# Redistributing a weight-quantization side stream over the four attention tiles of a two-layer transformer kernel

## What is computed

```python
xn = layernorm(x)
# layer 0: causal-weighted linear attention plus an int4-quantized linear layer with LoRA
scores    = (xn Wq^T)(xn Wk^T)^T * scale * exp(log_decay * dist) * causal
x = x + (scores @ (xn Wv^T)) Wo^T * out_scale + xn @ int4(kernel) + bias + (xn a) b
xn = layernorm(x)
# layer 1: decayed linear attention plus a feed-forward layer with ternary weights
Wq1, Wq2 = clip(round(W / (mean|W| + eps)), -1, 1)      for W1 (4096x1024), W2 (1024x4096)
x = x + attention(xn) + relu(xn Wq1^T + b1) Wq2^T + b2
```

## Time and profile before

| | us |
|---|---|
| two timed runs | 1556.30, 1684.81 (median 1620.56) |
| profiled execution, its time | 1558.54 |
| its span, slowest core (core 3) | 1557.0 |
| spans of the other seven cores | 1527.7 to 1549.3 |
| layer-0 attention, tile 0 to the start of layer 1 | 375.3 to 780.5 |
| PE busy | 1241.0 (80%) |
| ACT busy | 474.3 (30%) |
| DVE busy | 417.9 (27%) |

### The profile page before, as it was taken

How to read it: one execution, slowest core, us unless ns; L and a number is a source line. 1 busy time by engine, 2 the same in 40 slices (tenths; PEclk the granted TensorE clock), 3 DMA queues, 4 the chain that set the end, 5 groups by cost and what they waited for, 6 DMA issues and landing times. The chain is left out here.

```text
span 1557.0 us, 15405 instructions; the slowest of 8 cores (1527.7 to 1557.0 us)
## 1 busy us (share of the span) xinstructions
PE 1241.0 (80%) x5440; PEld 534.8 (34%) x5440; DVE 417.9 (27%) x704; ACT 474.3 (30%) x550; POOL 137.6 (9%) x184
## 2 busy tenths in 40 slices
PE   0276179996578577794729999999997999999997
PEld 0022034442233232331304444444443444444443
DVE  1498336001222332433247410030002200041000
ACT  0564023334543552634203332013202141032400
POOL 2331100000111111111110000000000000000000
PEclk9988679998789788897969999999998999999999
DMA  8796863002443654737495253353334152252423
GB/s 198 106 167 107 117 99 55 1 1 82 127 141 111 225 175 130 243 118 231 148 140 103 72 184 98 111 209 126 95 119 188 37 150 75 108 189 68 122 109 108
DMA packets 74202, 194.42 MB, mean 125 GB/s; under 512 B 8272, under 2 KB 16496, under 8 KB 69776
## 3 DMA queue, kind: packets, MB, share of 16 engines
q0 software_dynamic: 37072, 105.34, 28.5%
q1 hardware_dynamic: 37056, 88.09, 17.8%
HBM read 195.57 MB, written 33.56 MB: 147 GB/s over the span
## 5 line engine op out<-in xcount | busy, mean ns | idle before, releaser
L1214 PE MATMUL pb<-bigA,wqA 128*128 128x512 bf16 x1024 | 226.2, 379 | 0.0
L1174 PE MATMUL pb<-xn,xbf 128*128 128x512 bf16 x1024 | 222.5, 380 | 0.5 <-DMA xbf<-W1qS 0.5
L1157 PE MATMUL pb<-stm,bigB 128*128 128x512 bf16 x640 | 148.3, 395 | 54.1 <-DVE xa_bf L1012 37.7
L1101 ACT ACTIVATE bigA<-pb,cstF 128x512 bf16<-128x512 f32 x128 | 99.5, 777 | 218.7 <-PE pb L1174 218.7
L1047 DVE SCALAR_TENSOR_TENSOR xf<-pb,cstF,xf 128x512 f32<-128x512 f32 x32 | 24.0, 751 | 480.2 <-PE pb L1214 480.2
L1196 PE MATMUL pb<-rt,projW 128*128 128x512 bf16 x512 | 127.9, 395 | 29.9 <-DVE rt L1017 25.4
L1174 PEld LDWEIGHTS pb<-xn,xbf 128*128 128x128 bf16 x1024 | 100.1, 98 | 122.4 <-issue 1.0
L1214 PEld LDWEIGHTS pb<-bigA,wqA 128*128 128x128 bf16 x1024 | 100.2, 98 | 120.8
L1157 PEld LDWEIGHTS pb<-stm,bigB 128*128 128x128 bf16 x640 | 63.6, 101 | 139.1 <-issue 70.4
L429 PE MATMUL pb<-rt,cstB 128*128 128x512 bf16 x112 | 35.3, 446 | 83.9 <-DVE rt L395 83.9
L1089 ACT ACTIVATE statsT<-xbf,cstF 128x1024 bf16<-128x1024 f32 x46 | 57.0, 1240 | 118.6 <-DMA xbf<-W2T 78.5
(11 more groups left out here) (129 smaller groups left out, 1132.1 us busy)
## 6 DMA issues: line engine op xcount, KB each, us to landing
wqA<-W2qS POOLq DMA_DIRECT2D x32, 1024.0 KB, 6.1
xbf<-W1qS SPq DMA_DIRECT2D x128, 256.0 KB, 2.7
xbf<-W2T SPq DMA_DIRECT2D x28, 512.0 KB, 4.1
xbf<-W1T SPq DMA_DIRECT2D x18, 512.0 KB, 5.1
bigA<-W2T POOLq DMA_DIRECT2D x32, 256.0 KB, 9.2
bigA<-W1T POOLq DMA_DIRECT2D x16, 512.0 KB, 9.9
xf<-xT SPq DMA_DIRECT2D x4, 2048.0 KB, 9.1
x1S<-xf POOLq DMA_DIRECT2D x4, 2048.0 KB, 8.4
```

Of the source, the lines that this page charges most:

```text
L1101: got = si(s.activation(bigA[:, fc * 512:(fc + 1) * 512], pb[fc % 2][:, :], AF.Relu, bias=biasL[:, 48 + fc:49 + fc], scale=sc[:, C_Q4:C_Q4 ...
L1157: got = ti(t.matmul(bank[:, :], bigB[:, i * 1024 + ec * 128: i * 1024 + (ec + 1) * 128], stm[:, i * 512:(i + 1) * 512], start=(n == 0), st ...
L1174: got = ti(t.matmul(bank[:, :], xbf[:, (fc % 4) * 1024 + dc * 128: (fc % 4) * 1024 + (dc + 1) * 128], xn[:, p0:p0 + TS], start=(dc == 0), ...
L1214: got = ti(t.matmul(bank[:, :], wqA[:, (dc % 2) * 4096 + fc * 128: (dc % 2) * 4096 + (fc + 1) * 128], bigA[:, fc * 512:(fc + 1) * 512], st ...
```

## The change

One table of numbers is replaced: how many units each of the four layer-0 tiles takes.

```diff
         if layer == 0:
-            QUC = [10, 9, 7, 6]
+            QUC = [7, 10, 8, 7]
             u0 = sum(QUC[:j])
             units_j = list(range(u0, u0 + QUC[j]))
             NH = 2 * len(units_j)
```

## The result

The changed kernel takes 0.9923 of the time of the one before, 95% interval [0.9911, 0.9935], 12.0 us less by the ratio; the medians of all runs are 1544.49 us (11 runs) and 1555.93 us (10 runs). The ratio leaves out one disturbed run of each kernel, 1752.57 and 1684.81, and the latter had made the median of 1620.56 that stood ahead of the prediction. The forecast was -9.7 us.

A forecast was written before the change was run, and what follows sets the result against it. PE's waits for the weight stream, through DVE's order, were taken to bound layer-0 attention. By tiles, -20.9 + 2.8 + 2.9 + 5.5 = -9.7 us from 1558.54 gave 1548.8, say 1549; forecast 1543 to 1555 (0.55), range 1536 to 1561.

The forecast's parts named there:

- The bound: Layer-0 attention: no bandwidth or engine fills it; PE is held up by the weight stream, through DVE's order.
- Tile 0, up to xa: Six halves ahead of xa in place of nine, so PE starts R 17.0 us earlier.
- Tile 0, R: No block of R waits for a half; 3.9 us gained in R, 20.9 in all up to res.
- Tile 0, res: The res stage, PE alone for 32.6 us, stays so: nothing is won.
- Tile 1: 20 halves for 18: the last R block waits for q13 and not q12, so res starts 2.8 us later.
- Tile 2: 16 halves for 14: the last R block waits for q9 and not q8, 2.9 us later.
- Tile 3: 14 halves for 12: the last R block waits for q7 and not q5, 5.5 us later.
- The steps 3.75 and 3.58: Time in us from one half to the next, read from line L999 in tiles 2 and 3.
- C: Rival, slower: each added half puts its whole step on PE's path, 23.3 us lost, total 1561 to 1565; chance 0.15.
- Most of either is not bytes: In a 512 KB load (4.1 us) and a 256 KB store (3.2), the fixed part rules; twice the bytes cost 0.9 more.
- A: Rival: later tiles hide their added halves, only tile 0's 20.9 us counts, total 1537.6 or a little lower; chance 0.2.
- B: Rival: the stream is bound by bytes, the 64 halves take their time wherever they stand, total 1558.5; chance 0.1.

The follow-up runs named there:

- two-slot run: Changed kernel with two slots in every tile, where tiles 1 to 3 had 3, 4 and 4; 1.0380 of the kernel before, median 1613.59 us.
- late-six run: Kernel before, but tile 0's last six of 20 halves taken only after its last res block, one DVE drain added; 1.0034 of its time.

## Why the prediction was right

- **The bound.** The holes of layer-0 attention are waits for the stream through DVE's order. Shown by the two-slot run: nothing changed but the number of slots, and attention grew by 70 us.
- **Tile 0, up to xa:** -17.0 forecast, -17.6 by the medians.
- **Tile 0, R:** 3.9 forecast, 3.9 measured (21.5 less 17.6). On core 3 alone R lasts 30.51 and not 29.41, and the two stages up to res give 19.3 and not 20.9.
- **Tile 0, res:** I had it unchanged at 32.6; it lasts 31.0. The first 8 matmuls take 1.89 where they took 3.51, PE having been idle for 1.01 us ahead of them and not 4.73; the granted clock over them is 1.00 (447.50 to 449.40) where it was 0.53 (471.40 to 474.90), and that of the stage 1.00 for 0.95. This is the mis-sized term: 1.6 us of gain that a shorter wait brings besides its own length. It was missing from the step "Nothing is won".
- **Tile 1:** +2.8 forecast, +4.1 measured. 3.5 of them are there at the first res block, where the index rule held; the rest, 0.6, is lost in res, which I had named and put at nothing.
- **Tile 2:** +2.9 and +2.9, but only the sum agrees: 2.1 of it are there at the first res block, where I had all of it, and 0.8 come in res, where I had nothing. **Tile 3:** +5.5 and +6.5, of which 6.2 up to res.
- **The steps and the bytes.** The steps 3.75 and 3.58 were read too long, since they take in halves that wait for places in res; the forecasts go by q9's and q7's own times and are untouched, but the bounds 7.5 and 7.2, and C's price with them, were too high. "Most of either is not bytes" was wrong for the loads; no term of the sum hangs on it.
- **The sum:** -9.7 forecast, -9.5 by tiles. Two errors of some 2 us cancel (-2.1 in tile 0, +2.3 in the others), and that they do is luck. The ratio says -12.0, with an interval from -10.1 to -13.8. What it has beyond the tiles is not in the parts after attention (772.2 and 772.0); ahead of it the two profiled executions differ by 1.5 us in code that is the same. Whether the rest is that, or their scatter, was not tried.
- **Rivals.** A (later tiles free) falls, as each grew. B (bytes) falls by the two-slot run. C (whole steps) falls by the runs that moved all units to one tile: 2.8 of 4.3 and 2.2 of 3.6. But its mechanism is real: it holds for the halves ahead of the last R block, and in the late-six run six halves cost 4.4 each, above the 3.5 at which C decides. B has a grain too, the longer loads with four slots.

## What to carry to other kernels

When a side stream is woven by hand into an in-order engine, its price is not its work but the wait for the item that stands ahead of the place the main path needs: count that item's index, multiply by the step of its slots, and move items to where slots are many. Ask next what makes the step: here the slot was held through a store, and the first load stood behind a store and a 2 MB load that nobody needed yet. Moving such a wait to another buffer helps where its turn over its number of copies is shorter than before: two Sign pairs in place of two slots gained 6.6 us, and in place of four they lost 9.9 and 7.1.

## What the runs showed of the hardware

- A wait of PE of 1.01 us left the next 8 matmuls at 1.89 us (0.236 each), one of 4.73 us had them at 3.51 (0.44 each). The same pair, 1.01 and 1.89, stands in the two-slot run. The granted clock over these 8 is 1.00 in the one case and 0.53 in the other, the 2.4 GHz level and near the 1.2 GHz level. So the wait of 1.01 us cost its length, and that of 4.73 some 1.6 us more.
- A load of 256 KB lands in 2.9 to 3.4 us and one of 512 KB in 4.3 to 5.2, with eight cores loading and two to four slots in use. The Trainium skill, "DMA: Bandwidth & Descriptors", section "Anatomy of one DMA — SWDGE (gpsimd) path", would have the second 256 KB at 0.6 us, as an estimate by its bytes over 436 GB/s. Its figures are for DMAs that GpSimd issues, and these loads are issued by SP; for them the measured 1.4 to 1.8 decide.
- In the changed kernel weights of `W1` load more slowly than those of `W2` at the same size, 5.2 for 4.3 us. The rows of `W1` are 16 KB apart and not 4, but that by itself is not the reason: with two slots in every tile `W1` takes 3.5 us and `W2` 4.0. `W1` is loaded almost wholly in tiles 2 and 3, where four slots are in use.
